# A conditional residual chain on one core: products over 128 rows, four row transfers in place of eight, and both tables contracted over 128 rows

## The reference, cut to what matters

```
x = x + conv(x, weight0, pad 4, groups 4) + (cond @ c_weight.T)[:, :, None] + bias[None, :, None]
for n in 1, 2, 3:
    h   = gelu(cond @ W0 + b0);  h = gelu(h @ W1 + b1)
    att = softmax(h @ W2 + b2)                       # (128 samples, 8)
    agg_w = einsum('bk,koi->boi', att, weight_n)     # a 64x64 matrix for each sample
    agg_b = att @ bias_k
    x = x + einsum('boi,bih->boh', agg_w, x) + agg_b[:, :, None]
```

## Time and profile before

| | us |
|---|---|
| median of 3 runs | 355.47 (355.37 to 357.07) |
| the profiled execution's own time | 353.64 |
| its span, first to last instruction | 351.3 |
| granted TensorE clock, mean over the span | 0.988 |

### The profile page before, as it was taken

The page is one execution under the profiler, slowest core; times in us unless marked ns, Lnnn a source line. Parts: engine busy times, 40 slices in busy tenths (PEclk is TensorE's granted clock), DMA queues, the critical chain, the costliest instruction groups (busy, mean ns, idle before and its releaser), DMA issues.

```text
span 351.3 us, 5508 instructions
## 1 busy us (share of the span) xinstructions
PE 332.2 (95%) x1452; PEld 263.5 (75%) x1452; DVE 256.3 (73%) x250; ACT 235.1 (67%) x368; POOL 109.3 (31%) x110
## 2 busy tenths in 40 slices
PE   5999886899999999999999999999999999999983
PEld 5487574688888887887787888788888778788862
DVE  5255187388888878778888887888886796878674
ACT  5253278367777777777777777777777777777562
POOL 3050055513333323322232443143333113144400
PEclk9999999699999999999999999999999999999999
DMA  8849825069998999899999899989899989997658
GB/s 208 154 76 107 193 98 210 33 240 359 352 366 336 347 353 362 334 376 334 354 335 366 325 371 346 374 331 379 329 349 345 367 325 363 343 353 292 275 201 328
DMA packets 30395, 104.39 MB, mean 297 GB/s; under 512 B 3353, under 2 KB 4633, under 8 KB 22426
## 3 DMA queue, kind: packets, MB, share of 16 engines
q1 hardware_dynamic: 30388, 104.30, 84.4%
HBM read 36.13 MB, written 33.55 MB: 198 GB/s over the span
## 4 chain that ended last, share of the span: by engine, by line
PE 79%; DMA 9%; DVE 3%; issue 3%; SPq 2%; ACT 1%; POOL 1%; DVEq 0%; POOLq 0%
PE bank L387 47%; PE bank L423 9%; PE bank L425 8%; PE bank L424 8%; DMA x_sb<-in_x 5%; PE bank L395 4%; DMA ybuf<-conv_sb 3%; PE bank L436 2%; DMA early<-in_pairs 2%; SPq L280 1%; PE bank L494 1%; DVE table L774 1%; POOL a_dup L344 1%; ACT x_hi L553 1%; ACT conv_sb L560 1%
## 5 line engine op out<-in xcount | busy, mean ns | idle before, releaser
L560 ACT ACTIVATE conv_sb<-bank 128x512 f32<-128x512 f32 x128 | 76.5, 598 | 68.2 <-PE bank L387 64.1
L676 DVE TENSOR_TENSOR x_lo<-x_sb,x_hi 128x2064 fp32r<-128x2064 f32 x29 | 66.9, 2309 | 39.6 <-ACT x_hi L553 39.6
L387 PE MATMUL bank<-x_hi,toep_hi 128*128 128x512 f32 x256 | 85.7, 417 | 4.6 <-issue 3.5
L387 PE MATMUL bank<-x_hi,toep_lo 128*128 128x512 f32 x256 | 81.6, 400 | 0.0
L387 PE MATMUL bank<-x_lo,toep_hi 128*128 128x512 f32 x256 | 81.6, 400 | 0.0
L344 POOL COPY a_dup<-table 128x256 f32 (+1 forms) x32 | 26.8, 838 | 168.8 <-PE bank L395 166.4
L690 DVE TENSOR_TENSOR ybuf<-ybuf 128x2048 fp32r<-128x2048 f32 x31 | 70.9, 2286 | 0.1
L553 ACT ACTIVATE x_hi<-x_sb 128x2064 fp32r<-128x2064 f32 x32 | 61.6, 1925 | 12.7 <-DMA x_sb<-in_x 12.6
L349 POOL COPY a_diag<-table 64x128 f32 (+1 forms) x64 | 65.0, 1016 | 9.4 <-POOL a_diag L349 4.7
L580 ACT ACTIVATE out_sb<-bank,beta 128x512 f32<-128x512 f32 x93 | 63.7, 687 | 4.4 <-DMA out<-out_sb 1.4
L387 PEld LDWEIGHTS bank<-x_hi,toep_lo 128*128 128x128 f32 x256 | 49.1, 192 | 12.3
(11 more groups left out here) (78 smaller groups left out, 227.7 us busy)
## 6 DMA issues: line engine op xcount, KB each, us to landing
x_sb<-in_x SPq DMA_DIRECT2D x32, 1032.0 KB, 7.8
ybuf<-conv_sb SPq DMA_DIRECT2D x128, 256.0 KB, 4.6
out<-out_sb SPq DMA_DIRECT2D x30, 1024.0 KB, 7.9
out_sb<-conv_sb SPq DMA_DIRECT2D x8, 128.0 KB
out<-out_sb SPq DMA_DIRECT2D x4, 256.0 KB, 3.5
out<-x_sb SPq DMA_DIRECT2D x4, 256.0 KB, 3.8
x_sb<-in_toep SPq DMA_DIRECT2D x1, 640.0 KB, 5.7
early<-in_mixrow SPq DMA_DIRECT2D x1, 390.0 KB
```

Source lines behind the costliest of these rows:

```text
L387: last = mm(o, w[:, d, g, :], v[:, par, g, :, d:d + J], start=i + d == 0, stop=i + d == 3)
L560: nc.scalar.activation(conv_sb[:, par, g, :], conv_ps[g % banks][:, :], ACT.Copy).then_inc(conv_out, 1)
L676: nc.vector.tensor_tensor(x_lo[:, par].rearrange("p g s j -> p (g s j)"), x_sb[:, par].rearrange("p g s j -> p (g s j)"), x_hi[:, par].rea ...
```

## The change

1. Products over 128 rows: `pairs` is loaded into all 128 partitions (1280 columns, 640 KB in place of 256 KB). The upper 64 rows hold the operands for l = 4 to 7, the lower for l = 0 to 3. The operands are arranged so that a product sums over 128 rows with zeros in the rows that don't belong, and l and l + 4 stand side by side in the result's rows. There are 8 matmuls of 256 columns in place of 4 of 512.
2. Their rows travel in four DMAs of 256 KB, each to 16 rows, every eighth partition, in 2 KB runs.
3. The rows of table 0 get a buffer of their own (table 1's space, free until t = 8) and are spread over every fourth partition; both tables contract over all 128 rows. What isn't used is zero: POOL clears one buffer (128x4096), DVE the other (128x4096 in place of 32x4096). `coef` has 256 columns and is turned by two transposes.
4. SP issues `pairs` ahead of `toep`; DVE's operation on `toep` stands behind the coefficients; bias product 0 goes from t = 3 to 4, bias turn 0 from t = 6 to 7.

```diff
-BIAS_PRODUCTS = (3, 8, 12)
-BIAS_TURNS = (6, 11)
+BIAS_PRODUCTS = (4, 8, 12)
+BIAS_TURNS = (7, 11)
-CB = 16
-ROWS = ((IDENT3 - K, IDENT3 + 1), (0, LAYER3))
+RS = 4
+OWN = 2
+CB = 8
+LQ = K // 2
 def pair_row(l):
-    return (l // 4) * 64 + (l % 4) * K
+    return l // 2 + RS * (l % 2)
...
-        mrow = out_sb[:].rearrange("p q s n -> p (q s n)")
+        mrow = [table[1][:].rearrange("p b c -> p (b c)"), out_sb[:].rearrange("p q s n -> p (q s n)")]
...
+            sp.dma_start(pairs, pairs_h).then_inc(pairs_in, 16)
             sp.dma_start(toep_all, toep_h).then_inc(toep_in, 16)
-            sp.dma_start(pairs, pairs_h).then_inc(pairs_in, 16)
             sp.dma_start(ident[:], kept_h).then_inc(kept_in, 16)
-            sp.dma_start(mrow[LAYER3:LAYER3 + K], own_h[0:K]).then_inc(rows3_in, 16)
-            sp.wait_ge(rows_zero, 1)
-            sp.dma_start(mrow[IDENT21:IDENT3 + 1:IDENT3 - IDENT21], own_h[K:K + 2]).then_inc(rows3_in, 16)
+            sp.wait_ge(rows3_zero, 1)
+            sp.dma_start(mrow[0][0:RS * K + 1:RS], own_h[0:K + 1]).then_inc(rows3_in, 16)
             load(0, 0)
-            sp.dma_start(mrow[OWN:OWN + 2 * K], own_h[K + 2:]).then_inc(rows21_in, 16)
+            sp.wait_ge(rows21_zero, 1)
+            sp.dma_start(mrow[1][OWN:RS * 2 * K:RS], own_h[K + 1:3 * K + 1]).then_inc(rows21_in, 16)
...
-            for l in (0, 4, 1, 5, 2, 6, 3, 7):
-                sp.dma_start(mrow[pair_row(l):pair_row(l) + K].rearrange("m (a n) -> m a n", a=CB),
+            for l in range(LQ):
+                sp.dma_start(mrow[1][pair_row(l)::2 * RS].rearrange("m (a n) -> m a n", a=CB),
                              prod[:, l].rearrange("p c k -> p (c k)")).then_inc(rows21_in, 16)
...
+            nc.gpsimd.memset(mrow[0], 0.0).then_inc(rows3_zero, 1)
...
-                mm(prod_bank[g][:, :], pair1[:, g, :], pair2, start=True, stop=True).then_inc(pprod_ps, 1)
+                for c in range(2):
+                    last = mm(prod_bank[g][:, LQ * C * c:LQ * C * c + LQ * C], pair1[:, 2 * g + c, :], pair2,
+                              start=True, stop=True)
+                last.then_inc(pprod_ps, 1)
...
-                    last = mm(t_bank[t % TB][:, B * i:B * i + B], mrow[rows, at:at + 2 * C], coef_t[rows, :],
+                    last = mm(t_bank[t % TB][:, B * i:B * i + B], mrow[n][:, at:at + 2 * C], coef_t[:, n, :],
...
-            nc.vector.memset(mrow[32:64, :], 0.0).then_inc(rows_zero, 1)
+            nc.vector.memset(mrow[1], 0.0).then_inc(rows21_zero, 1)
```

More of the change, by code:

```diff
@@ L129, in cond_resid_kernel @@
         at = EARLY["net"] + EARLY["mixrow"]
-        pairs = early_sb[0:C, at:at + EARLY["pair1"] + EARLY["pair2"]]
-        pair1 = early["pair1"][0:C].rearrange("j (c n) -> j c n", c=4)
-        pair2 = early["pair2"][0:C]
+        pairs = early_sb[:, at:at + EARLY["pair1"] + EARLY["pair2"]]
+        pair1 = early["pair1"].rearrange("j (c n) -> j c n", c=CB)
+        pair2 = early["pair2"]
         ident = sb("ident", [128, 128])
@@ L151, in cond_resid_kernel @@
         mix_f = sb("mix_f", [128, S * G, 2, CG])
-        coef = mix_f[:].rearrange("b a r o -> b (a r o)")[:, 0:128]
-        coef_t = sb("coef_t", [128, B])
+        coef_all = mix_f[:].rearrange("b a r o -> b (a r o)")[:, 0:NT * 128]
+        coef = coef_all.rearrange("b (t r) -> b t r", t=NT)
+        coef_own = coef_all.rearrange("b (t i s) -> b t i s", t=NT, s=RS)
+        coef_t = sb("coef_t", [128, NT, B])
         vrow = sb("vrow", [B, C])
@@ L329, in _ @@
         def _(pool):
+            nc.gpsimd.memset(mrow[0], 0.0).then_inc(rows3_zero, 1)
+            pool.wait_ge(rows3_zero, 1)
             nc.gpsimd.memset(ones[:], 1.0).then_inc(ones_set, 1)
             nc.gpsimd.memset(vcol[:], 1.0).then_inc(ones_set, 1)
-            nc.gpsimd.memset(coef, 0.0).then_inc(coef_zero, 1)
+            nc.gpsimd.memset(coef_all, 0.0).then_inc(coef_zero, 1)
             pool.wait_ge(coef_zero, 1)
-            nc.gpsimd.memset(coef[:, IDENT21:IDENT3 + 1:IDENT3 - IDENT21], 1.0).then_inc(coef_zero, 1)
+            for t, at in enumerate((RS * K, OWN + RS * 2 * K)):
+                nc.gpsimd.memset(coef[:, t, at:at + 1], 1.0).then_inc(coef_zero, 1)
             nc.gpsimd.memset(a3_diag[:], 0.0).then_inc(zeros_set, 1)
@@ L469, in _ @@
             pe.wait_ge(kept_in, 16)
-            pe.wait_ge(coef_zero, 2)
-            pe.wait_ge(coef_set, 3)
-            nc.tensor.transpose(bank[3][:, 0:B], coef, ident[:]).then_inc(coef_t_ps, 1)
+            pe.wait_ge(coef_zero, 3)
+            pe.wait_ge(coef_set, 4)
+            for t in range(NT):
+                last = nc.tensor.transpose(bank[3][:, B * t:B * t + B], coef[:, t], ident[:])
+            last.then_inc(coef_t_ps, 1)
             for g in range(2, 4):
                 pair_products(g)
-            pe.wait_ge(rows3_in, 32)
+            pe.wait_ge(rows3_in, 16)
             pe.wait_ge(coef_t_set, 1)
@@ L748, in _ @@
                                     ALU.mult).then_inc(att_set, 1)
-            dve.wait_ge(coef_zero, 2)
+            dve.wait_ge(coef_zero, 3)
             dve.wait_ge(att_set, 1)
[L752 to L758, removed]
+            for e in range(2):
+                both = coef[:, 1, C * e:C * e + C].rearrange("b (m u v) -> b m u v", u=2, v=RS)[:, :, :, 0:2]
+                of_l = att[:, 1, LQ * e:LQ * e + LQ].rearrange("b (o v u) -> b o u v", o=1, u=2)
+                of_m = att[:, 0, :].rearrange("b (m o p) -> b m o p", o=1, p=1)
+                nc.vector.tensor_tensor(both, of_l.to_broadcast([B, K, 2, 2]), of_m.to_broadcast([B, K, 2, 2]),
+                                        ALU.mult).then_inc(coef_set, 1)
+            nc.vector.tensor_copy(coef_own[:, 1, 0:2 * K, OWN], att[:, 0:2, :].rearrange("b n k -> b (n k)")).then_inc(coef_set, 1)
+            nc.vector.tensor_copy(coef_own[:, 0, 0:K, 0], att[:, 2, :]).then_inc(coef_set, 1)
+            dve.wait_ge(toep_in, 16)
+            taps = toep.rearrange("p (d g m) -> p d g m", d=2, g=G)
+            eyes = eye_tap.rearrange("p (d o m) -> p d o m", d=2, o=1)
+            nc.vector.tensor_tensor(taps, taps, eyes.to_broadcast([128, 2, G, 128]), ALU.add).then_inc(toep_set, 1)
             dve.wait_ge(coef_t_ps, 1)
-            nc.vector.tensor_copy(coef_t[:], bank[3][:, 0:B]).then_inc(coef_t_set, 1)
+            nc.vector.tensor_copy(coef_t[:], bank[3][:, 0:NT * B].rearrange("r (t b) -> r t b", t=NT)).then_inc(coef_t_set, 1)
             dve.wait_ge(c0_ps, 2)
@@ L883 @@
     }
+    pairs = np.zeros((2, C, CB * 128 + LQ * C), f)
+    for e in range(2):
+        first = pairs[e, :, 0:CB * 128].reshape(C, RS, 2, 2, K, CB)
+        first[:, :, :, e] = ws[0][:, :, at].reshape(K, C, 2, CB, RS).transpose(1, 4, 2, 0, 3)
+        pairs[e, :, CB * 128:] = ws[1][LQ * e:LQ * e + LQ].transpose(2, 0, 1).reshape(C, LQ * C)
+    pairs = pairs.reshape(128, -1)
     biask = np.stack([a[p + "bias_k"].reshape(K * C) for p in mixes])
@@ L892 @@
                                   biask[None]]),
-        "pairs": np.concatenate([
-            ws[0][:, :, at].reshape(K, C, 2, CB, 2).transpose(1, 4, 2, 0, 3).reshape(C, 4 * 128),
-            ws[1].transpose(2, 0, 1).reshape(C, K * C)], 1),
-        "own": np.concatenate([table_rows(ws[2].transpose(0, 2, 1)), table_rows(eye[None, :, at]), table_rows(eye[None]),
-                               table_rows(ws[0][:, :, at]), table_rows(ws[1][:, :, at])]),
+        "pairs": pairs,
+        "own": np.concatenate([table_rows(ws[2].transpose(0, 2, 1)), table_rows(eye[None]),
+                               table_rows(ws[0][:, :, at]), table_rows(ws[1][:, :, at]), table_rows(eye[None, :, at])]),
     }
```

26 lines of the change are left out of this document (12 added, 14 removed).

## The result

| | before | changed |
|---|---|---|
| median of the runs, us | 355.37 | 336.81 (335.09 to 345.31) |
| ratio to before | | 0.952, interval 0.942 to 0.963 |
| profiled execution: its time, span, clock | 353.64, 351.3, 0.988 | 345.31, 343.2, 0.967 |

The change gains 18.6 us where 12 were forecast (343.5), and the time lies under the range's lower end, 339.5. The ratio and its interval leave out, on both sides, the executions more than 1.5% above their kernel's fastest, so it is not the quotient of the two medians. The direction and the two mechanisms were as forecast; the size was not.

What follows compares the result with a forecast made beforehand. The prediction took the queued load of x(1), with TensorE's low clock as second brake, to bound the kernel before 61.5 us. Between -11.4 and -13.3 it took -12: 341.6 us, 343.5 on the median's scale, range 339.5 to 352.

Steps and rivals of the forecast that it cites:

- the two mechanisms: Product rows land faster, bringing x(1) at 28.8 instead of 42.4; dense 128-row products raise TensorE's clock, 0.97 a table step.
- late case: TensorE's clock rises at 18 to 21 us; last table copy at 50.1 against 61.54, -11.4.
- the early one: TensorE's clock rises already during the first products, so everything behind products 2 and 3 moves 1.9 earlier: -13.3.
- The steps on the transfer: Four issues in place of eight, product rows at 210 GB/s in 5.0 us, x(1) landing at 28.8 instead of 42.4.
- the moved turn: Bias chain: vcol now comes behind x_high(1), and TensorE waits for it ahead of the third convolution: +1.6.
- The rival of a slow x(1): x(1) load slow for its own reason, still 17.4 us from issue: -1.6, 353.8 us; chance 0.08.
- The one of a shared port: Product rows' transfer: every eighth partition meets at one port, x(1) 20 us later than now, 375 us; chance 0.06.
- the term on the clock: Table prologue: the 128-row products raise TensorE's clock; the sum is -11.4 for a late rise, -13.3 for an early one.
- The passage behind the tables: After the last table copy, TensorE idles 3.5 us and its clock falls; expected the same again, a microsecond either way.
- The rival "the clock doesn't rise": TensorE's clock stays low until the first convolution, table steps at 1.71 us: -3.9, 351.6 us; chance 0.18.

Runs made afterwards that it cites:

- again: The changed kernel profiled once more with no edit: 333.23 us for the profiled execution, median of all six 338.78 us.
- free: The changed kernel, but POOL's x_lo(0) also waits for toep_lo and the bias sum's last reduction writes PSUM: 336.47 us.
- nearf: `free` with the 16 rows of each transfer as neighbours, not every eighth partition: 341.20 us.
- near8f: `free` with the product rows in eight DMAs, each to 8 neighbouring rows, in 2 KB runs: 343.65 us.
- fuse: `free` with the last bias addition writing vdup straight from vrow and PSUM: 332.62 us.
- best: `fuse` with ACT's x_high(1) also moved from behind t = 7 to behind t = 8: 329.51 us.
- both64: The changed kernel with products over the lower 64 rows only and table 0 over its 36 used rows: 347.46 us.
- prod64f: `free` with products over the lower 64 rows only, tables still over 128 rows: 337.49 us.
- tab36f: `free` with table 0 over its 36 used rows instead of 128, products still over 128 rows: 340.55 us.
- eightf: `free` with the product rows in eight DMAs, each to 8 rows, still every eighth partition: 342.58 us.

## Why the prediction was wrong

Measured against the profile of `again`, where the clock was up from the start, and, for a late rise, that of `free`. The forecast's column is its late case; for the early one it took 1.9 off each moment behind the products:

| step | forecast | again | free |
|---|---|---|---|
| products start | 8.3 | 7.9 | 8.3 |
| first issue of the product rows | 19.2 | 13.7 | 17.8 |
| issues of the rows until x(1) | 2.6 | 2.6 | 2.6 |
| ACT's x_high(1) ends | 31.3 | 26.9 | 28.6 |
| from there to the last table copy | 18.8 | 18.6 | 18.3 |
| last table copy ends | 50.1 | 45.5 | 47.0 |
| from there to the span's end (before 289.8) | as before | 285.7 | 288.3 |

The steps on the transfer held. Issues, the rate (forecast 210 GB/s; 282 in the window above, 250 in `again` from 15.8 to 18.8), x(1) landing 6.2 and 8.6 us after its issue (forecast 7.0), and the stretch behind x_high(1), 17.2 and 1.6 for the moved turn, are right within 2 us. In that stretch TensorE waited 1.76 us for vcol in `again` but 0.33 in `free`. The rival of a slow x(1) falls with nearf and near8f: x(1) takes 12.0 and 15.8 us where the rows ahead of it are slow, and 6.2 where they are not. The one of a shared port falls with the 282 GB/s of `free`: every eighth partition is the fast case.

What failed are two terms of the sum, which together put 12 us where the spans give 16.0 (`free`) and 20.1 (`again`). The larger is the term on the clock: "a clock that rises late, at 18 to 21 us", -11.4, with -13.3 for a rise "already during the first products". Measured, the last table copy came 14.6 us sooner in `free` and 16.0 in `again`. The sum let only the products raise the clock, since in the one profile at hand the net's matmuls ahead of them had not. They can: in `again` both halves of the products run at 2.4 GHz; the rows and x(1) are issued 3.6 us ahead of even the early case, and the last table copy comes 2.7 ahead of it, since x(1), among others, took 1.6 us longer to land than the forecast had. In `free`, where the rise came during the second half, the issue is 1.4 us ahead of the late case: 0.7 because the last products, too, are partly fast (3.11 for 3.78), 0.5 because the second transpose, put at 0.4, cost nothing that shows. In all profiles with 128-row products the clock was up by about 17.5, where the late case of the forecast put it at 18 to 21.

The second is "The passage behind the tables ... comes again the same", put at nothing. From the last table copy on, `free` gained another 1.4 us and `again` 4.1. The passage up to the first product of the mixing took 9.0 us before, 6.7 in `again` and 6.8 in `free`; the loop behind it took 280.8, 279.0 and 281.5. The clock does not fall in the passage of `again`, and in that of `free` it is back by 50.4, after 3 us of work. The windows from the last table copy on (clock is the third figure from the end), before and in `again`:

```profile
61.50:76.00 14.50, 13.02 (x49) 10.35 (x50) 7.95 (x8) 6.22 (x11) 6.43 (x12) 0.76 0.41 146
```
```profile
46.00:60.00 14.00, 12.52 (x59) 10.00 (x58) 9.15 (x7) 8.31 (x15) 6.49 (x12) 1.00 0.48 171
```

TensorE idles 3.5 us in both:

```profile
61.63 0.71 PE L387 MATMUL bank<-x_hi,toep_hi 128*128 128x512 f32 x2 [3.46 <-issue]
```
```profile
45.63 0.70 PE L397 MATMUL bank<-x_hi,toep_hi 128*128 128x512 f32 x2 [3.47 <-issue]
```

Why the same idle time costs the clock in one and not in the other, no run tested, and it stays open, as does the 1.8 to 2.5 us by which the loops differ. In `fuse` and `best`, where the idle time is 1.8 us, the clock does not fall.

A third matter was not in the prediction at all: DVE and POOL hold each other up. It worked against the gain and so is no reason for the miss. It costs some 10 us in the executions of the upper heap (4 of 11) and sets the spread of the changed kernel; `free` shows it by removing it. The agreement within 2 us of single steps is no proof of the sum: the first profile, with its meetings, ended its tables at 55.3.

The rival "the clock doesn't rise" was the right counterpart. both64, which nearly makes it true, came out at 347.5, 11.0 us over `free` in the same batch and 4 us under that rival's time; in its profile half of the products still ran fast (1.99 us for 3.78), which would be 1.8 of the 4.

So of the 17.6 us of `free`, the clock and the transfer each carry a part and neither carries it alone: without the clock both64 keeps 6.6, without the transfer near8f (which also lacks the meetings) keeps 11.6. The two parts overlap, and these differences don't add up.

## What to carry to other kernels

Before counting on a wait's length, count what stands ahead in the same queue, and look at the destination rows: spread partitions and 16 rows in a transfer gave 282 GB/s where 8 neighbours gave 74. In a prologue of small matmuls read the clock from the records' durations; here a contraction padded with zero rows to 128 cost TensorE nothing (1.70 us for a step at 1.2 GHz, over 9 rows before and over 128 in `prod64f`) and let it run at twice the pace. Where executions of one kernel fall in two heaps, look for one engine's short operation that ends exactly with another's long one, and change its inputs or its place.

## What the runs showed of the hardware

- **DVE operations with two SBUF inputs and POOL's exclude each other.** With two SBUF inputs, DVE's toep_lo took 5.05 us beside POOL's subtraction and 1.22 alone; the 64-column addition 4.37 or 0.23, and 0.22 beside POOL with one input in PSUM. A 128-column copy was held too (1.48 against 0.23), and POOL's copy by DVE's subtraction (2.41 against 0.40). Whoever starts first keeps its pace. Not held were DVE's table copies out of PSUM and its reduction of `mix_f` from SBUF (1.05 us beside x_lo(2) in `again`, 1.02 alone). The Trainium skill (SBUF — State Buffer, Who interferes with whom) says this: a DVE instruction with two SBUF inputs contends with a GpSimd one that reads SBUF, and the later one blocks until the first has finished. The trace agrees, and the prediction should have drawn on it. The held copy has one SBUF input and lies outside that sentence.
- **Rows of zeros count for the clock.** Over 128 rows, 119 of them zero, it rose and stayed up (prod64f); over 36 it fell (tab36f), with TensorE as busy.
- **The clock's first rise differs between executions**: by 6.7 us in `again` and both64, at about 16.5 in `free`, and once up and down again (first profile).
- **16 DMA engines show as a share of 1.06, transfers to eight rows as 0.53 to 0.57 (eightf, near8f)**: they left half of the DMA's engines idle or, before the change, to the load queued behind them.
